# Int8-style MLP in a transformer layer: quantized activations in four tiles instead of one, and weight staging through one DMA queue instead of two

## The reference, cut to what matters

```python
def _weight_quant(w):
    scale = 1.0 / jnp.clip(jnp.mean(jnp.abs(w)), 1e-05)
    return jnp.clip(jnp.round(w * scale), -1.0, 1.0) / scale
def _act_quant(x):
    scale = 127.0 / jnp.clip(jnp.max(jnp.abs(x), axis=-1, keepdims=True), 1e-05)
    return jnp.clip(jnp.round(x * scale), -128.0, 127.0) / scale
def _bitlinear(x, w):
    return jnp.einsum('bsi,oi->bso', _act_quant(x), _weight_quant(w))

x = x + attention(layernorm(x))            # Wqkv (3072, 1024), Wproj (1024, 1024)
h = layernorm(x)
gate = silu(_bitlinear(h, w_gate))         # (4096, 1024)
up = _bitlinear(h, w_up)                   # (4096, 1024)
x = x + _bitlinear(gate * up, w_down)      # (1024, 4096)
```

## Time and profile before

| what | value |
|---|---|
| median of 2 timed runs | 6254.32 us (6230.17 to 6278.46) |
| the profiled execution's own time | 6010.31 us |
| its span (core 3, the slowest; the others 5952.4 to 6004.8) | 6008.7 us |
| busy in that span: TensorE matmuls, VectorE, ScalarE | 4536.6, 2738.6, 2205.9 us |
| weight staging: until attention's first transpose (L315) | 0 to 480.7 us |
| of that, pass one: sum of a piece (L547), first and last start | 34.5 to 215.9 us, 3617 ns each |
| attention, L315 first and last | 480.7 to 2473.1 us |
| gate and up, L488 first and last | 2673.0 to 5060.2 us |
| down, L518 first and last | 5111.7 to 5998.4 us |

### The profile page before, as it was taken

One profiled execution on the slowest core, in us unless ns is written; L12 is line 12 of the kernel. 1 busy time (PEld: TensorE's weight loads), 2 busy tenths in 40 slices (PEclk: granted clock), 3 DMA queues, 4 the chain that ended last, 5 costly groups with the idle time before them and its releaser, 6 DMA issues.

```text
span 6008.7 us, 86498 instructions; the slowest of 8 cores (5952.4 to 6008.7 us)
## 1 busy us (share of the span) xinstructions
PE 4536.6 (76%) x28932; PEld 2165.2 (36%) x28932; DVE 2738.6 (46%) x5280; ACT 2205.9 (37%) x5274; POOL 110.7 (2%) x175
## 2 busy tenths in 40 slices
PE   0006777777777777738888888888888886999999
PEld 0003333333333333413444444444444443444444
DVE  0374343344443434436666666666666664111111
ACT  3203444445444444524444444444444443000000
POOL 0010000000000000000000000000000000000000
PEclk9998777777777787769999999999999998999999
DMA  9891110000001100040111111111111112444444
GB/s 260 299 311 54 38 49 29 29 29 29 29 29 47 39 29 29 15 144 36 43 43 43 43 43 43 43 43 43 43 43 43 43 39 94 150 151 152 154 154 133
DMA packets 94687, 467.14 MB, mean 78 GB/s; under 512 B 8115, under 2 KB 8244, under 8 KB 65588
## 3 DMA queue, kind: packets, MB, share of 16 engines
q1 hardware_dynamic: 51828, 243.48, 12.6%
q0 software_dynamic: 33472, 167.79, 7.5%
q10 hardware_dynamic: 8960, 50.33, 2.4%
HBM read 310.58 MB, written 159.38 MB: 78 GB/s over the span
## 4 chain that ended last, share of the span: by engine, by line
PE 56%; DVE 16%; ACT 10%; issue 7%; DMA 6%; DVEq 3%; another core or an unknown queue 1%; SPq 0%; ACTq 0%; POOL 0%; POOLq 0%
PE pb L518 15%; PE pb L326 12%; PE pb L488 10%; PE pb L496 10%; PE pb L382 6%; ACT esb L615 4%; DVE m_sb L909 3%; DVE hq_tm L911 3%; DMA stage<-wgT 2%; PE pb L474 1%; ACT L669 1%; ACT u_sb L672 1%; DVE ln L833 1%; DVE ln L832 1%
## 5 line engine op out<-in xcount | busy, mean ns | idle before, releaser
L488 PE MATMUL pb<-wgq_sb,xq_fm 128*128 128x512 bf16 x4096 | 1052.8, 404 | 79.9 <-ACT xq_fm L656 79.9
L496 PE MATMUL pb<-wuq_sb,xq_fm 128*128 128x512 bf16 x4096 | 987.0, 384 | 0.0
L518 PE MATMUL pb<-wdq_sb,hq_in 128*128 128x512 bf16 x4096 | 887.0, 380 | 37.4 <-DMA hq_in<-hq_scr 37.4
L326 PE MATMUL pb<-xn_fm,wqkvT_sb 128*128 128x512 bf16 x3072 | 704.2, 394 | 28.1 <-ACT xn_fm L572 28.1
L886 DVE SCALAR_TENSOR_TENSOR m_sb<-u_sb,agm,silug 128x512 f32<-128x512 f32 x512 | 382.8, 748 | 500.5 <-ACT u_sb L672 500.2
L496 PEld LDWEIGHTS pb<-wuq_sb,xq_fm 128*128 128x128 bf16 x4096 | 409.1, 100 | 513.1 <-issue 53.2
L518 PEld LDWEIGHTS pb<-wdq_sb,hq_in 128*128 128x128 bf16 x4096 | 401.4, 98 | 522.7 <-issue 41.4
L488 PEld LDWEIGHTS pb<-wgq_sb,xq_fm 128*128 128x128 bf16 x4096 | 395.8, 102 | 501.3 <-issue 172.7
L669 ACT ACTIVATE silug<-pb,agm 128x512 f32<-128x512 f32 x512 | 357.3, 698 | 333.2 <-PE pb L488 215.7
L934 DVE SCALAR_TENSOR_TENSOR out_sb<-pb,gam,xnsub 128x512 f32<-128x512 f32 x128 | 96.2, 751 | 832.1 <-PE pb L518 832.1
L326 PEld LDWEIGHTS pb<-xn_fm,wqkvT_sb 128*128 128x128 bf16 x3072 | 308.7, 101 | 418.7 <-issue 81.7
(11 more groups left out here) (123 smaller groups left out, 5005.0 us busy)
## 6 DMA issues: line engine op xcount, KB each, us to landing
xnsub<-xnew_scr SPq DMA_DIRECT2D x128, 512.0 KB, 3.4
hq_scr<-hq_fm POOLq DMA_DIRECT2D x64, 1024.0 KB, 4.2
hq_in<-hq_scr SPq DMA_DIRECT2D x64, 1024.0 KB, 7.4
x_sb<-x SPq DMA_DIRECT2D x16, 2048.0 KB, 11.4
xnew_scr<-xnew POOLq DMA_DIRECT2D x16, 2048.0 KB, 13.6
out<-out_sb POOLq DMA_DIRECT2D x64, 512.0 KB, 8.1
stage<-wgT ACTq DMA_DIRECT2D x16, 1024.0 KB, 13.3
stage<-wgT SPq DMA_DIRECT2D x16, 1024.0 KB, 13.5
```

Source lines behind the costliest of these rows:

```text
L326: ins = t.matmul(P[2 + c % 2][:], wqkvT[:, m * 3072 + c * 128: m * 3072 + (c + 1) * 128], xn_fm[:, m * 512:(m + 1) * 512], start=(m == 0), ...
L488: ins = t.matmul(P[[2, 3, 0][jg % 3]][:], xq_fm[k % 2][:, m * 128:(m + 1) * 128], wgq[:, m * FI + pc * 512: m * FI + (pc + 1) * 512], star ...
L496: ins = t.matmul(P[[4, 5, 1][jg % 3]][:], xq_fm[k % 2][:, m * 128:(m + 1) * 128], wuq[:, m * FI + pc * 512: m * FI + (pc + 1) * 512], star ...
L518: ins = t.matmul(P[j % 4][:], hq_in[k % 2][:, m * 128:(m + 1) * 128], wdq[:, m * 1024 + pc * 512: m * 1024 + (pc + 1) * 512], start=(m == ...
```

## The change

There are two edits. The first takes the halves away: SyncE's queue loads each whole piece in one DMA of 2 MB, ScalarE's queue loads nothing, and the two drains and the DMA issues on ScalarE go, as do four semaphores. The second gives the rounded activations four tiles `hq4[0..3]` of 128 x 1024 at the places where `hq_tm` lay (the memory is the same 8 KB for each partition). The rounding runs in four quarters of 1024 columns, with a count of `v_hq` for each, and the quarter q waits only until the transposes that read that quarter of the subtile before have been done.

```diff
@@ sync_body
             for j in range(NPC):
-                psrc, dstv = stage_half(j, 0)
+                psrc, _, w = piece_desc(j)
+                dstv = stage[j % 2][:, 0:w]
...
                 sync.dma_start(out=dstv, in_=psrc).then_inc(SM[f"s_stg{j % 2}"], 16)
@@ hqT in tensor_body
-                t.wait_ge(SM["v_hq"], 2 * k + (1 if b < 4 else 2))
+                t.wait_ge(SM["v_hq"], 4 * k + b // 2 + 1)
...
+                hsl = hq4[(4 * k + b // 2) % 4]
                 for kk in range(4):
-                    j = b * 4 + kk
+                    j = (b % 2) * 4 + kk
                     ins = t.matmul(P[6 + b % 2][:, kk * 128:(kk + 1) * 128],
-                                   hq_tm[:, j * 128:(j + 1) * 128], c_id[:],
+                                   hsl[:, j * 128:(j + 1) * 128], c_id[:],
@@ scalar_body
                 sc.wait_ge(SM[f"s_stg{j % 2}"], 16 * (j // 2 + 1))
-                sc.wait_ge(SM[f"s_stg{2 + j % 2}"], 16 * (j // 2 + 1))
...
-                if j + 2 < NPC:
-                    sc.drain()
-                    ps, dv = stage_half(j + 2, 1)
-                    sc.dma_start(out=dv, in_=ps).then_inc(SM[f"s_stg{2 + j % 2}"], 16)
-            sc.drain()
-            for j in range(NPC):
-                if j >= 2:
-                    sc.wait_ge(SM["v_stg"], j - 1)
-                ps, dv = stage_half(j, 1)
-                sc.dma_start(out=dv, in_=ps).then_inc(SM["s_st2b" if j % 2 == 0 else "s_st2d"], 16)
@@ vector_body, pass two
-                v.wait_ge(SM["s_st2a" if j % 2 == 0 else "s_st2c"], 16 * (j // 2 + 1))
-                v.wait_ge(SM["s_st2b" if j % 2 == 0 else "s_st2d"], 16 * (j // 2 + 1))
+                v.wait_ge(SM["s_st2a" if j % 2 == 0 else "s_st2b"], 16 * (j // 2 + 1))
@@ b1_m in vector_body
-                if k >= 1:
-                    v.wait_ge(SM["t_hqT"], 8 * k)
-                for hh in range(2):
-                    hs = slice(hh * 2048, (hh + 1) * 2048)
+                for qq in range(4):
+                    if k >= 1:
+                        v.wait_ge(SM["t_hqT"], 8 * (k - 1) + 2 * (qq + 1))
+                    hs = slice(qq * 1024, (qq + 1) * 1024)
                     TS(m_sb[:, hs], m_sb[:, hs], ln2[:, L + 43:L + 44], MAGIC, ALU.mult, ALU.add)
                     v.drain()
-                    TS(hq_tm[:, hs], m_sb[:, hs], MAGIC, None, ALU.subtract).then_inc(SM["v_hq"], 1)
+                    TS(hq4[qq][:], m_sb[:, hs], MAGIC, None, ALU.subtract).then_inc(SM["v_hq"], 1)
                     v.drain()
```

More of the change, by code:

```diff
@@ L99, in build_nc @@
         sem_names = [
-            "s_wa", "s_wag", "s_stg0", "s_stg1", "s_stg2", "s_stg3", "s_st2a", "s_st2b", "s_st2c", "s_st2d", "s_qo0", "s_qo1", "s_x0", "s_x1", "s_wb1", "s_wb2",
+            "s_wa", "s_wag", "s_stg0", "s_stg1", "s_st2a", "s_st2b", "s_qo0", "s_qo1", "s_x0", "s_x1", "s_wb1", "s_wb2",
             "s_xno0", "s_xno1", "s_xni0", "s_xni1", "s_xni2", "s_hqo0", "s_hqo1", "s_hqia", "s_hqib", "s_xnia", "s_xnib",
@@ L188, in build_nc @@
         m_sb = at("m_sb", [128, FI], F32, 158 * KB)
-        hq_tm = at("hq_tm", [128, FI], BF16, 174 * KB)
+        hq4 = [at(f"hq_tm{i}", [128, 1024], BF16, 174 * KB + 2 * KB * i)
+               for i in range(4)]
         hq_fm = [at(f"hq_fm{i}", [128, FI], BF16, 182 * KB + 8 * KB * i) for i in range(2)]
@@ L205, in sync_body @@
             for j in range(NPC):
-                psrc, dstv = stage_half(j, 0)
+                psrc, _, w = piece_desc(j)
+                dstv = stage[j % 2][:, 0:w]
+                if j >= 16:
+                    dstv = dstv.rearrange("p (s f) -> p s f", s=4)
                 if j >= 2:
@@ L211, in sync_body @@
             for j in range(NPC):
-                psrc, dstv = stage_half(j, 0)
+                psrc, _, w = piece_desc(j)
+                dstv = stage[j % 2][:, 0:w]
+                if j >= 16:
+                    dstv = dstv.rearrange("p (s f) -> p s f", s=4)
                 if j >= 2:
                     sync.wait_ge(SM["v_stg"], j - 1)
-                sync.dma_start(out=dstv, in_=psrc).then_inc(SM["s_st2a" if j % 2 == 0 else "s_st2c"], 16)
+                sync.dma_start(out=dstv, in_=psrc).then_inc(SM["s_st2a" if j % 2 == 0 else "s_st2b"], 16)
             for i in range(nt):
@@ L522, in tensor_body @@
                         ins.then_inc(SM["t_d"], 1)
[L524 to L534, removed]
         def scalar_body(sc):
[L537 to L540, removed]
             for j in range(NPC):
```

## The result

| what | before | after |
|---|---|---|
| median of the timed runs | 6209.5 us (6006.94 to 6278.46, 10 runs) | 6340.34 us (6166.45 to 6511.27, 11 runs) |
| lowest run | 6006.94 us | 6166.45 us |
| the profiled execution's own time | 6010.31 us | 6234.89 us |
| attention's first transpose | 480.7 us (mean of the eight cores 476.6) | 467.3 us (mean of the eight cores 472.5) |
| gate and up: mean turn of VectorE's rounding | 37.45 us | 39.96 us |

The changed kernel is slower: the ratio is 1.0261, 95% interval 1.0232 to 1.0291, which is about 157 us on 6010. In most executions of either kernel the cores of a die are held at a lower clock for a part of the time (in the profiled one of after, core 2 stands at 0.82 from 6000 to 6050 us where core 4 stands at 1.00), so the ratio and all that follows go by the executions and cores without that.

What follows compares the result with a forecast made beforehand. It took the VectorE, ScalarE and TensorE chain through the rounding in gate and up as the bound. 73 (rounding) + 30 (clock) + 0 (one queue) = +103 us, giving 6357 us, range 6245 to 6405.

Steps and rivals of the forecast that it cites:

- the slowdown that was given 0.25: Whole kernel: chance 0.25 that the change is slower by over 2%, the least a measurement can tell.
- The chain through VectorE, ScalarE and TensorE: Gate and up: rounding delays statistics, square root, silu and TensorE's third transpose; statistics wait rises from 10.6 to about 12 us.
- Rounding in quarters: VectorE's rounding in gate and up: extra instructions, drains and waits cost +1.2 us a turn, 61 times, 73 us.
- What the edit gives: Gate and up: earlier transposes worth at most 0.8 us in 57 turns; not waiting for the last transposes worth nothing.
- What the longer stall does to the clock: TensorE in gate and up: 17 or 18 more turns pay 1.68 us for the low clock, +30 us (-59 to +44).
- two places: TensorE's low clock in a turn: after the stall, costing 1.68 us, or on the subtile's first gate group, costing nothing.
- One queue, 0 us: Staging passes: whole pieces on one queue cost 0 us, with bounds of 0 and 34 us.
- 465 to 495 allowed: Sign for the first edit: its 0 is wrong if attention starts before 465 or after 495 us.
- The clock absorbs it: Gate and up: longer turns put the low clock before the stall nearly always; +14 us, 6268 us; chance 12%.
- One queue is slower: Staging: 24 pieces each land 1.4 us later on one queue; +137 us in all, 6391 us; chance 13%.
- staging speeds up: Pass two: writes get a larger share of the DMA engines, 15 us less; +88 us, 6342 us; chance 5%.
- the hand-off pays: Gate and up: TensorE's late transposes set the stall, so earlier quarters gain; -18 us, 6236 us, or -48 us; chance 4%.

Runs made afterwards that it cites:

- dead instruction of 1.31 us: Kernel before, rounding still in halves, plus one VectorE multiply by 1.0 of 2048 unused columns behind the rounding; lowest 6164.45 us, turn 39.9 us.
- the first run: Kernel before with only the first edit, whole pieces on SyncE's queue and rounding still in halves; ratio 1.0009 (0.9999 to 1.0019).
- the second: Kernel before with only the second edit, rounding in quarters with four waits and pieces still halved on two queues; ratio 1.0263, lowest 6167.25 us.
- the kernel with quarters and early inputs: Changed kernel with statistics and square root moved into the blocks, next input's transposes between block 6's gate and up matmuls; ratio 0.9659, lowest 5800.43 us.
- the run with 1440 columns: Kernel before plus one VectorE multiply by 1.0 of 1440 columns behind the rounding, 0.99 us more path a turn; ratio 1.0073, turn 38.2 us.

## Why the prediction was right, and where its size was off

The direction and the bound were right, and the measured median of 6340 us lies in the range; that it is 17 us from the forecast is partly luck, since the medians of the two kernels were 203 and 174 us above their lowest runs. Like for like the loss was forecast at 103 us (1.7%) and is 157 us (2.6%), so the slowdown that was given 0.25 is what happened. By the prediction's steps:

- **The chain through VectorE, ScalarE and TensorE.** Right. ScalarE's wait was forecast at about 12 us and is 12.0. The dead instruction of 1.31 us showed that only the chain's length counts here.
- **Rounding in quarters, +1.2 us a turn, 73 us.** Nearly right: +1.31 and 80 us. The durations of 0.75 and 0.69 us are as worked out; a wait costs 0.07 us and not 0.04, three of them 0.1 us more.
- **What the edit gives: nothing.** Right for this kernel, and a statement about the stall more than about quarters: where TensorE did wait for the rounding, quarters gave 1.6 us a turn.
- **What the longer stall does to the clock, +30 us with a bound of +44.** This is the step that failed. It measured +78 us. The step counted turns, at a fixed price of 1.68 us, and took it that each turn has one low stretch in one of two places. The count was too low: 27 more turns pay, all 61, where the forecast had 17 or 18 more and its bound 26; at 1.68 us that makes 45 us, not 30. The larger part is the price: 33 turns pay 2.9 us, for a stretch twice as long, 1.2 us more than the forecast's price and about 40 us together. (The two make 85; the short stretches behind the longest stalls cost 1.35 us and not 1.68, which takes some of it back.) Nor are the two places alternatives: where the clock is low ahead of a stall that has shrunk to 3.6 us, it is low behind it as well. The bound was drawn from two stall lengths, and the change went outside the lengths that the trace had shown.
- **One queue, 0 us.** Right within what the time can tell: 1.0009, and attention began at 467 us on core 4, inside the 465 to 495 allowed. On the mean of the cores it began some 4 us earlier.
- **The rivals.** "The clock absorbs it" was wrong for this change and right about its condition: it was to decide under about 1.0 us, and at 0.41 us the loss is within 7 us, at 0.99 us it is 44 where the path alone makes 60. "One queue is slower" falls with the first run, as does "staging speeds up" in its size of 15 us; "the hand-off pays" falls with the second.

The rule weighed from the Trainium skill, "TensorE: Matmul & The Clock Gate", section "Why this matters for your kernels", that idle gaps between bursts of matmuls cost the clock, told the direction: all 61 stalls are followed by 1.2 GHz. It was used for a count alone, with 117 us as its sum; that falls short for the same reason as the forecast, the price of a turn.

The rule from the Trainium skill, "DMA: Bandwidth & Descriptors", section "Queues, rings and completion order", by which two queues instead of three would speed the writes up, would have given up to 15 us. The time of the run with one queue alone shows none of it (its interval starts at 0.01% faster), and pass two draws 316 GB/s before and 317 after. The 3 us by which pass two is shorter go the way of the rule, at a fifth of that size; no run shows that the writes' share is the reason.

## What to carry to other kernels

Cutting an instruction in pieces for an earlier hand-off pays only where a row shows the consumer waiting for that producer; anywhere else the fixed cost of the pieces (here 1.31 us for four instructions, four drains and three waits) goes on whatever chain the producer is part of. Where that chain ends in a stall of TensorE of 3 to 5 us, the price of a small delay is not its length. Measure two or three lengths of a dead instruction, since here the first 0.4 us cost nothing and the last 0.3 cost a hundred. And before a stall is tuned, ask which early work of another item stands in the chain: moving LayerNorm's statistics and the transposes to where their engines had room gave 7%, with no operation made faster.

## What was not expected of the hardware

- The stretch at 1.2 GHz comes in two lengths. In the changed kernel it lasted 6.5 us or more behind 33 stalls of core 4 and about half as long behind the other 28; the earlier trace rows have 3.25 us only. Behind stalls of the same 5.25 us both occur: the long ones began 0.83 us or more before the stall's end, the short ones 0.80 us or less.
- The length of a stall alone does not tell whether the low clock follows it. It also follows two waits of 1.35 and 1.19 us with a group of short transposes between them, and one wait of 2.34 us in every turn of the kernel with quarters and early inputs, while the stalls of 3.25 us shown in the run with 1440 columns were not followed by it; there a low stretch had begun 16 us before the stall's end.
- A wait that is already satisfied, behind a drain on VectorE, costs 0.07 us (a gap of 0.16 us where a drain alone left 0.09).
